# Last cross-attention of a decoder: TensorE's program takes the key blocks by twos

## The reference

```python
x = _layernorm(x, ln_media_w, ln_media_b)          # the context, 77 rows
lat = _layernorm(latents, ln_lat_w, ln_lat_b)      # x of the decoder, 512 rows
q = lat @ Wq + bq
kv_in = jnp.concatenate([x, lat], axis=1)
k, v = jnp.split(kv_in @ Wkv + bkv, 2, axis=-1)
...
sim = jnp.einsum('bhid,bhjd->bhij', q * scale, k)
sim = sim - jax.lax.stop_gradient(jnp.max(sim, axis=-1, keepdims=True))
attn = jax.nn.softmax(sim, axis=-1)
out = jnp.einsum('bhij,bhjd->bhid', attn, v)
...
return out @ Wout + bout
```

## Time and profile before

| | |
|---|---|
| median of 3 runs | 1187.98 us (1183.43 to 1190.98) |
| the profiled execution | 1186.95 us, its span 1185.2 us |
| TensorE busy in the span | 92% (6794 matmul instructions) |
| VectorE, ScalarE, GpSimd busy | 63%, 51%, 13% |

### The profile page before, as it was taken

The page is one execution under the profiler, slowest core; times in us unless marked ns, Lnnn a source line. Parts: engine busy times, 40 slices in busy tenths (PEclk is TensorE's granted clock), DMA queues, the critical chain, the costliest instruction groups (busy, mean ns, idle before and its releaser), DMA issues.

```text
span 1185.2 us, 18015 instructions
## 1 busy us (share of the span) xinstructions
PE 1089.3 (92%) x6794; PEld 916.4 (77%) x6794; DVE 742.8 (63%) x1736; ACT 605.3 (51%) x1125; POOL 152.9 (13%) x115
## 2 busy tenths in 40 slices
PE   6779999999997568999999999999999999999896
PEld 4558778888887347888889888889888898889532
DVE  5854766566565766877665676665757657563246
ACT  5235544342335436666654665564656546563353
POOL 6110220027626220002000000000000000000001
PEclk9956858999998668999999999999999999999998
DMA  6100000000001000000000000000000000000001
GB/s 222 7 1 1 1 1 1 1 1 1 1 1 36 1 1 1 2 1 2 2 1 2 2 1 2 2 1 2 2 1 2 1 1 2 1 1 2 1 0 36
DMA packets 15680, 10.11 MB, mean 9 GB/s; under 512 B 8759, under 2 KB 14827, under 8 KB 15083
## 3 DMA queue, kind: packets, MB, share of 16 engines
q1 hardware_dynamic: 15595, 8.96, 2.6%
HBM read 7.60 MB, written 1.05 MB: 7 GB/s over the span
## 4 chain that ended last, share of the span: by engine, by line
PE 72%; ACT 15%; DVE 8%; issue 5%; POOL 1%; DMA 0%; POOLq 0%; ACTq 0%; DVEq 0%
PE PS L1414 67%; ACT KA L864 8%; ACT BIG L884 4%; PE PS L1426 4%; PE PS L1783 1%; DVE st L926 1%; DVE X_ODD L937 1%; DVE mxm L1301 1%; DVE BIG L1020 0%; DVE mx L1017 0%; DVE X_EVEN L937 0%; ACT BIG L682 0%; ACT BIG L674 0%; DVE mv L929 0%; DVE REG L960 0%
## 5 line engine op out<-in xcount | busy, mean ns | idle before, releaser
L1414 PEld LDWEIGHTS PS<-VXA,BIG 128*128 128x128 f32 (+1 forms) x3136 | 396.6, 191 | 47.4 <-ACT BIG L884 23.1
L1414 PE MATMUL PS<-VXA,BIG 128*128 128x65 f32 (+2 forms) x3136 | 398.8, 272 | 8.9 <-ACT BIG L884 8.9
L884 ACT ACTIVATE BIG<-PS 128x512 f32<-128x512 f32 (+1 forms) x320 | 187.2, 594 | 180.2 <-PE PS L1414 177.2
L1301 DVE TENSOR_REDUCE mxm<-PS 128x1 f32<-128x512 f32 x256 | 170.6, 688 | 85.8 <-PE PS L1414 81.6
L864 ACT ACTIVATE KA<-PS,b1s 64x512 fp32r<-64x512 f32 (+1 forms) x256 | 128.4, 502 | 49.7 <-PE PS L1414 44.0
L1414 PE MATMUL PS<-QA,KA 128*128 128x512 f32 (+1 forms) x320 | 144.9, 453 | 0.0
L557 POOL TENSOR_TENSOR rs<-ve,half_neg 128x4 f32<-128x4 f32 (+1 forms) x29 | 30.0, 1035 | 844.8 <-DVE ve L931 844.8
L1414 PE MATMUL PS<-QB,KB 128*128 128x512 f32 (+1 forms) x320 | 125.9, 394 | 0.0
L1414 PE MATMUL PS<-KA,QA 128*128 128x512 f32 (+1 forms) x512 | 116.7, 331 | 3.4 <-ACT KA L864 2.7
L1414 PEld LDWEIGHTS PS<-KA,QA 128*128 128x128 f32 x512 | 87.1, 190 | 24.5 <-DVE mxm L1301 3.5
L786 ACT ACTIVATE BIG<-PS 128x512 f32<-128x512 f32 x72 | 42.5, 596 | 94.6 <-PE PS L1414 94.2
(11 more groups left out here) (253 smaller groups left out, 1583.8 us busy)
## 6 DMA issues: line engine op xcount, KB each, us to landing
X_EVEN<-in_x SPq DMA_DIRECT2D x4, 256.0 KB, 4.0
VXA<-in_L_ffn_Wg SPq DMA_DIRECT2D x1, 1024.0 KB, 5.9
VXA<-in_L_ffn_Wu SPq DMA_DIRECT2D x1, 1024.0 KB, 7.8
VXA<-in_L_ffn_Wd SPq DMA_DIRECT2D x1, 1024.0 KB, 9.5
REG<-in_L_xattn_Wkv SPq DMA_DIRECT2D x1, 1024.0 KB, 5.0
QB<-crow SPq DMA_DIRECT2D x64, 2.0 KB
out<-X_EVEN SPq DMA_DIRECT2D x4, 256.0 KB, 2.3
wq1s<-in_L_xattn_Wq SPq DMA_DIRECT2D x1, 512.0 KB, 8.3
```

What stands on the lines that cost most here:

```text
L884: act.activation(PX[0:rows, g % 4, :], PS[0:rows, g % 2, :], ACT.Exp, scale=SCALE_W).then_inc(pw_ready, 1)
L1301: dve.tensor_reduce(mxm[:, p % 2, h, m:m + 1], PS[:, 2 + g % 2, :], AX.X, ALU.max).then_inc(mu_free, 1)
L1414: return pe.matmul(dst, lhsT, rhs, start=start, stop=stop, **kw)
```

## The change

TensorE's loop over the slots goes by twos: the scores of both slots, two of the units of both, the two pending `pv` (of the pair before), the other units, and the tasks of both slots. The programs of the other engines stay as they are.

```diff
--- before.py
+++ after.py
@@ -1796,15 +1796,20 @@
                     task(key)
             for p in range(STEPS):
                 tasks = step_tasks(p)
-                for slot in range(SLOTS):
+                for slot in range(0, SLOTS, 2):
                     s_wide(p, slot)
-                    if p + 1 < PAIRS:
-                        for u in MAX_UNITS.get(slot, []):
-                            max_unit(p + 1, u)
+                    s_wide(p, slot + 1)
+                    units = MAX_UNITS.get(slot, []) + MAX_UNITS.get(slot + 1, []) if p + 1 < PAIRS else []
+                    for u in units[0:2]:
+                        max_unit(p + 1, u)
                     if SLOTS * p + slot:
+                        pv(SLOTS * p + slot - 2)
                         pv(SLOTS * p + slot - 1)
-                    for key in tasks.get(slot, []):
+                    for u in units[2:]:
+                        max_unit(p + 1, u)
+                    for key in tasks.get(slot, []) + tasks.get(slot + 1, []):
                         task(key)
+            pv(SLOTS * STEPS - 2)
             pv(SLOTS * STEPS - 1)
             task(EPILOGUE[0])
```

## The result

The changed kernel takes 1291.8 us (median of four runs, 1278.1 to 1299.6) where the kernel before takes 1185.7 beside it: 1.091 times as long, 95% interval 1.084 to 1.098. The profiled execution took 1286.75 us (span 1285.0), 99.8 us more than the one of before.

What follows compares the result with a forecast made beforehand. The prediction took TensorE to bound the kernel, busy 92% of the span; 48.3 + 6.8 + 24 + 12.4 + 6 - 15.4 = 82 us on 1186.95 gave 1269, forecast 1270 us, bounds 1250 to 1290, stated range 1218 to 1295.

Steps and rivals of the forecast that it cites:

- the transfer: c's row going through DVE and two SP DMAs to the next step's slot 0: 0.5 us on 12 steps, 6 us.
- Regrouping worth nothing: TensorE's same matmuls taken by twos cost the same by themselves; bound 3 us either way.
- Wait (1): TensorE before slot 3's scores, for exp(1) queued behind Q's evacuation on ScalarE: 1.61 us in 30 steps, 48.3 us.
- Wait (2): TensorE at unit 8, for DVE's maxima queued behind the V copy: 0.38 us in 18 steps, 6.8 us.
- Waits (3) and (4): TensorE on DVE: before c, behind head_out, 24 us; before slot 7's V, for Kt's bank, 12.4 us.
- PE clock 1.00: Expected sign in the profile after: TensorE's granted clock stays at 1.00 in this stage.
- Rival B: Pauses in each step bring TensorE's clock down, 78 us on 30 steps: 1348 us, chance 0.06.
- A: Only the ScalarE wait is new, slack takes up DVE's waits: 1221 us, chance 0.09.
- C: Faster: exponentials a pair ahead leave nothing to wait for, 15 us come back: 1173 us, chance 0.03.
- D: New waits and old ones cancel: within 1% (12 us), chance 0.02.

Runs made afterwards that it cites:

- ScalarE's order changed: Changed kernel with ScalarE's exponential of slot 1 ahead of its evacuation of Q, hi(Q,0): 1225.3 us, 1.045 of the kernel before.
- the swap on DVE: Changed kernel with VectorE's maxima of units 5 and 6 ahead of the V copy of slot 2: 1298.1 us in one run.
- three reorderings: Changed kernel with exp(1) ahead of hi(Q,0), even head's head_out behind lo of K and Kt, maxima 5 and 6 ahead of V copy: 1177.4 us, 0.997 of before.

## Why the prediction was right, point by point

**Direction and mechanism** were right: four waits, the first by far the largest. The time came to 1291.8 us against 1270. That is within the stated 1218 to 1295, but above 1250 to 1290, the bounds of the sum, and at the very end of the 1245 to 1292 of the forecast alone. The upper bound stood for more work of DVE; that the time came near it through the clock instead is luck. The sum was 82 us; measured are 100 us on the profiled execution, 104 in the stage. The mis-sized term is the clock, put at nothing, 25 us. Without it the stage is 79.3 us longer, and the sum without the transfer and with the wait before yE, 82 - 6 + 3, is 79.

- **Regrouping worth nothing**: 16 instructions in 1.70 us against the forecast of 0.81 + 0.89. Shown again by the kernel with all pauses filled, whose stage is 79.3 us longer than before at a clock of 1.00, no more than the waits come to.
- **Wait (1)**: 2.22 us from Q's last matmul, 1.54 lost and 0.10 for the unhidden load (715.02 to 715.35 instead of 0.23), against 1.53 + 0.08. Shown by ScalarE's order changed (gone, 64 us, some 47 of them the wait) and by Q at slot 1 in the kernel before (29 us without any clock).
- **Wait (2)**: 0.4 us in a step with V, against 0.38. Place and price are shown by the swap on DVE, by its steps at full clock.
- **Waits (3) and (4)**: 2.52 us against 2.51 from `pv(4)` to c, 0.64 against 0.68 from c to V; with head_out moved 40 us gone, 36 of them waits, against 36.
- **The transfer** was overrated: 6 us were taken, 0.5 on each of 12 steps. A step without V grew by 1.95 us at full clock; the other terms give 1.86, with the transfer it would be 2.4. In the step above the row of c was written at 706.53 and slot 0's scores started at 708.82, 0.42 us behind the first transpose of oT, 0.37 in the kernel before. So both transfers had landed 2.3 us after the first issue; whatever wait remains is in the 4.7 us on "issue", at most 0.2 us a time. The landing time itself isn't shown. I had taken it from a transfer of 256 KB.
- **Not listed**: yE waits for the copy of oT, now directly ahead of it, 3 times 1.1 us.
- **The clock**: "PE clock 1.00" was wrong. Rival B had the mechanism, with a stretch at the lower level in every step (78 us, chance 0.06). It came in 9 of 31 steps (17 of 73 windows), for 25 us. I argued against it that the engine would be busy at 85%. The truth lay between forecast and rival, and the right reading of the earlier trace rows was some loss beside the forecast, not an alternative to it. What the Trainium skill tells of another kernel, in TensorE: Matmul & The Clock Gate, "A second HAM failure mode: psum-queue depth-cycling", agrees with this case: short idle times between groups of matmuls, and a clock that goes to and fro, 0.96 on average here.
- **Rivals A, C, D** are refuted: DVE's waits came in full although the pause lets it catch up, and nothing was faster.

## What to carry to other kernels

Where engines run fixed programs, moving a producer on one engine is a change to the place of every consumer in the other engines' queues; ask, for each moved instruction, what stands behind its consumer there. Here 104 us of loss in one stage became 10 us of gain by three reorderings on the engines that had been left alone. Removing one wait can uncover another that it had covered, so walk all queues again after each step, and price pauses on TensorE above their length: 79 us of waits cost 104 here. Their length alone doesn't say when.

## What the runs showed of the hardware that I had not expected

- **Pauses cost clock, but not all of them.** 58 pauses of the matmuls of at most 0.8 us (Q at slot 1) left the granted clock at 1.00. Pauses of 1.4 to 1.8 us, once per step of some 22 us, brought it to 0.97; with those before c and V added, 0.96. But length doesn't decide alone: where the pause at slot 3 was gone or filled, the clock still fell, in 5 and 7 windows, each time behind the pauses before c and V, of 0.6 and 0.4 us, c and V starting 0.64 us apart. Needless matmuls in the pauses brought it back to 1.00 and made the kernel faster. Which steps are hit isn't regular: most are not. What decides it stays open.
- **A part of the program that no kernel here changes varies.** The stretch up to the first row of c took 441.3 us in the kernel before and 422.9 us in the one with exp(6) ahead of Kt, with the same instructions (PE x2130):

```profile
0.00:441.30 441.30, 376.05 (x2130) 309.60 (x2131) 276.85 (x758) 178.84 (x373) 133.41 (x96) 0.84 0.06 18
```

```profile
0.00:422.90 422.90, 357.27 (x2130) 292.03 (x2131) 276.58 (x758) 178.48 (x373) 133.74 (x96) 0.89 0.07 19
```

The granted clock was 0.84 and 0.89 in them. These 18 us are 1.5% of the kernel and as much as any gain looked for here; the times of a stage between two fixed instructions tell more than the time of the whole.
